# Two attentions with plain 64x64 products in place of folded weights, and roundings and a normalising moved to ScalarE

## What is computed

```python
# L2 and L3 attention: 8 heads of 64 channels
q, k, v = layernorm(x) @ Wq, context @ Wk, context @ Wv
out = softmax(q k^T / 8) v @ Wo + bo        # per sequence and head
x = x + tanh(g_xattn) * out
# L2 FFN, every linear layer with weights in {-1, 0, 1} and inputs rounded to 8 bits
act_quant(x): scale = 127 / clip(max|x|, 1e-5); round(x * scale) / scale
h = square(relu(bitlinear(y, w_gate))) * bitlinear(y, w_up)   # y = layernorm(x)
x = x + tanh(g_ffn) * bitlinear(h, w_down)
# L3 FFN: square(relu(y @ A)) @ B, with A and B prepared from ternary weights
```

## Time and profile before

| | us |
|---|---|
| median of 3 runs | 1649.75 (1649.02 to 1652.42) |
| the profiled execution's own time | 1648.05 |
| its span, first to last instruction | 1646.3 |
| TensorE busy in the span | 1494.6 |
| VectorE busy | 1190.2 |
| ScalarE busy | 874.5 |
| GpSimd busy | 582.6 |
| mean granted TensorE clock | 0.934 of full speed |

### The profile page before, as it was taken

How to read it: one execution, slowest core, us unless ns; L and a number is a source line. 1 busy time by engine, 2 the same in 40 slices (tenths; PEclk the granted TensorE clock), 3 DMA queues, 4 the chain that set the end, 5 groups by cost and what they waited for, 6 DMA issues and landing times.

```text
span 1646.3 us, 43347 instructions
## 1 busy us (share of the span) xinstructions
PE 1494.6 (91%) x14329; PEld 1046.6 (64%) x14329; DVE 1190.2 (72%) x4951; ACT 874.5 (53%) x1741; POOL 582.6 (35%) x1120
## 2 busy tenths in 40 slices
PE   6999999988998779898889689989988999899998
PEld 5888888875665445454477456656655665566665
DVE  6777877766777799999837744436888888865554
ACT  5656666654554555555323255555566666655543
POOL 4455544540000666666136411103322232222221
PEclk9999999998999687888669889999999999999999
DMA  8000000006200000000010000000000000000000
GB/s 191 2 0 0 0 0 0 0 2 138 52 0 14 1 0 0 0 0 0 2 46 0 15 19 0 0 0 2 1 2 0 0 1 1 2 8 7 6 13 20
DMA packets 40363, 22.41 MB, mean 14 GB/s; under 512 B 23231, under 2 KB 37790, under 8 KB 40158
## 3 DMA queue, kind: packets, MB, share of 16 engines
q1 hardware_dynamic: 40286, 21.42, 5.5%
HBM read 17.22 MB, written 4.19 MB: 13 GB/s over the span
## 4 chain that ended last, share of the span: by engine, by line
PE 63%; DVE 21%; issue 8%; ACT 4%; POOL 2%; DVEq 1%; DMA 0%; POOLq 0%; ACTq 0%
PE ps L681 7%; PE ps L690 7%; PE ps L2099 5%; PE ps L2094 5%; DVE arena L1355 5%; DVE arena L1349 4%; PE ps L303 3%; PE ps L310 3%; PE ps L352 3%; PE ps L332 3%; PE ps L2149 3%; PE ps L2160 2%; PE ps L343 2%; PE ps L323 2%; PE ps L2138 2%
## 5 line engine op out<-in xcount | busy, mean ns | idle before, releaser
L2262 ACT COPY arena<-ps 128x512 f32<-128x512 f32 x128 | 75.1, 587 | 150.9 <-PE ps L2099 150.9
L2094 PE MATMUL ps<-arena 128*128 128x128 f32 x1024 | 138.2, 281 | 3.4 <-ACT arena L2299 3.4
L681 PE MATMUL ps<-xnT,arena 128*128 128x512 f32 x256 | 135.1, 621 | 0.0
L2099 PE MATMUL ps<-arena 128*64 128x512 f32 x512 | 135.0, 605 | 0.0
L2094 PEld LDWEIGHTS ps<-arena 128*128 128x128 f32 x1024 | 126.8, 196 | 4.9 <-ACT arena L2299 4.4
L2557 POOL TENSOR_TENSOR arena<-arena 128x512 f32<-128x512 f32 x64 | 67.9, 1061 | 130.5 <-DVE arena L2493 130.0
L574 POOL TENSOR_TENSOR ln_veps<-ln_mv,eps 128x4 f32<-128x4 f32 x40 | 10.8, 269 | 269.0 <-DVE ln_mv L568 269.0
L1813 DVE TENSOR_SCALAR_CACHE_REDUCE thr_hits<-thr_abs,thr_candidate 128x512 bf16<-128x512 f32 (+1 forms) x248 | 101.8, 477 | 0.0
L1355 DVE MATCH_REPLACE8 arena<-arena 128x64 f32<-128x64 f32 x512 | 101.7, 210 | 0.1
L830 DVE SCALAR_TENSOR_TENSOR x_res<-ps,arena,x_res 128x128 f32 (+1 forms) x256 | 72.0, 345 | 31.1 <-PE ps L690 28.5
L2256 ACT COPY arena<-ps 128x512 f32<-128x512 f32 x128 | 77.1, 605 | 29.2 <-PE ps L2094 28.8
(11 more groups left out here) (409 smaller groups left out, 3978.4 us busy)
## 6 DMA issues: line engine op xcount, KB each, us to landing
toeplitz<-ssm_toeplitz_scratch SPq DMA_DIRECT2D x2, 2048.0 KB, 18.1
ssm_toeplitz_scratch<-ssm_padded_kernel SPq DMA_DIRECT2D x1, 2048.0 KB, 11.3
out<-x_res SPq DMA_DIRECT2D x8, 256.0 KB, 2.3
arena<-ctx SPq DMA_DIRECT2D x2, 768.0 KB, 6.0
arena<-L_ffn_W SPq DMA_DIRECT2D x2, 512.0 KB
arena<-L_xattn_Wq SPq DMA_DIRECT2D x1, 512.0 KB, 6.2
x_res<-x SPq DMA_DIRECT2D x1, 512.0 KB, 7.6
arena<-L_xattn_Wo SPq DMA_DIRECT2D x1, 512.0 KB, 8.2
```

The source lines that it names most:

```text
L681: nc.tensor.matmul(ps[:, u % 3, :], w1[:, x, c * P:(c + 1) * P], xnT, start=True, stop=True).then_inc(h_full.sem, 1)
L2094: last = T_.matmul(ps[:, 1 - n, j * P:(j + 1) * P], folded[phase].mT[:, 4 * n + j, :], cg[:, s, :], start=True, stop=True)
L2099: last = T_.matmul(ps[64 * m:64 * m + 64, 4, :], cg[:, s, b * CTX:(b + 1) * CTX], folded[phase].wvo[:, m, :, :], start=True, stop=True)
L2262: S.copy(VW[:, r % 2, b, :, :].rearrange("p c d -> p (c d)"), ps[:, 4, :]).then_inc(v_laid.sem, 1)
```

## The change

The function `fold_weights` is gone, with its work on TensorE, ScalarE and GpSimd ahead of the layer-1 FFN. `attention_weights` only loads the weights; ScalarE multiplies Wo and bo by the gate at the start of the decoder. A tile's attention now has queries and keys (4 products of 128x128 each), scores and heads (16 products of 64x64 each), values (4 products of 256 columns) and y. ScalarE rounds h and the normalised group, and normalises the four tiles; GpSimd computes the bias for that (-mean * 1/sqrt) and adds bo to x. The order of the streams changes.

```diff
-        k.fold_pool(e)      # and k.fold_act(e), k.fold_pe(e)
+def attention_weights(k, io, name, wq, wk, wv, wo, bo, inputs, outputs, conv_part):
+    def sp(e):
+        e.wait_ge(k.conv_done.sem, k.conv_done.at(conv_part))
+        e.dma_start(w.q, io[wq]).then_inc(w.loaded.sem, 16)
...
@@ pe_step @@
         if 2 <= r < STEPS + 2:
             e.wait_ge(p_laid.sem, p_laid.at(t - 1))
+            e.wait_ge(v_laid.sem, v_laid.at(t - 1))
+            e.wait_ge(q_laid.sem, q_laid.at(t + 1 if r < STEPS else STEPS))
+            for c, b_, m, rows, toks in quarters():
+                out = slice(64 * (m ^ b_), 64 * (m ^ b_) + 64)
+                last = T_.matmul(ps[out, 1 + b_, c * SEQ:(c + 1) * SEQ], VH[rows, s, b_, c, :], PT[rows, c, toks], start=True, stop=True)
+            last.then_inc(o_full.sem, 1)
+        if attend(r):
+            e.wait_ge(k_laid.sem, k_laid.at(t + 1))
+            for c, b_, m, rows, toks in quarters():
+                last = T_.matmul(ps[toks, 3 + m, c * CTX:(c + 1) * CTX], QT[rows, c, toks], KT[rows, c, toks], start=True, stop=True)
+            last.then_inc(s_full.sem, 1)
+            values(e, s, phase)
+        if 2 <= r < STEPS + 2:
+            e.wait_ge(o_laid.sem, o_laid.at(t - 1))
             for c in range(C):
                 for m in range(2):
+                    last = T_.matmul(ps[64 * m:64 * m + 64, 0, 0:D], OT[:, m, c, :], w_o[:, m, c, :], start=(c == 0), stop=(c == C - 1))
             last.then_inc(y_full.sem, 1)
+        if ahead(r, 1):
+            e.wait_ge(s_sub.sem, s_sub.at(t + 1))
+            turn_xn(e, t + 1, o)
         if gates(r):    # gate and up products, then x_done, hT, qT, PT's transpositions, queries, keys, down
...
@@ act_step @@
+        if downs(r):
+            e.wait_ge(a_recip.sem, a_recip.at(t - F2))
+            e.wait_ge(hq_done.sem, hq_done.at(t - F2 - 1))
+            S.activation(hq[:], h[:], ACT.Identity, bias=magic[:, 0:1], scale=sh[:, 0:1]).then_inc(hr_done.sem, 1)
+        if 2 <= r < STEPS + 2:
+            copy_heads(e, t)
+        if norms(r, 1):
+            e.wait_ge(n_shift.sem, n_shift.at(b))
+            for j in range(GT):
+                last = S.activation(k.xn[:, 0, j, :], k.x[:, tile_at(t, r, j, 7), :], ACT.Identity, bias=n_bias[:, j:j + 1], scale=k.rstd[:, 0, j:j + 1])
+            last.then_inc(n_out.sem, 1)
         if attend(r):
+            copy_values(e, t, s)
+            S.activation(PR[:, s, :, :, :], PR[:, s, :, :, :], ACT.Exp, scale=SCALE).then_inc(s_exp.sem, 1)
+        if ahead(r, 1):
+            copy_xn(e, t + 1, o)
         if gates(r):    # relu, hT's copy, qT's copy, PT's copy, square, then copy_queries, copy_keys
...
+        if norms(r, 2) and r < LN3:
+            for j in range(GT):
+                last = S.activation(qf[:, j, :], k.xn[:, 0, j, :], ACT.Identity, bias=magic[:, 0:1], scale=sc[:, j:j + 1])
@@ dve_step @@
         if downs(r):
-            round_h(e, t)
+            scale_h(e, t)        # scale and its inverse only
...              # maximum and subtraction of the scores, then:
+        if downs(r):
+            clip_h(e, t)
...              # after h and its maximum:
+        if downs(r):
+            e.wait_ge(y2_full.sem, y2_full.at(t - F2))
+            V.scalar_tensor_tensor(k.x[:, u, :], ps[:, 6, 0:D], yc[:, 0:1], k.x[:, u, :], ALU.mult, ALU.add).then_inc(y2_done.sem, 1)
@@ pool_step @@
+            G_.tensor_tensor(n_mean[:], k.mv[:, 0, :, 0], k.rstd[:, 0, :], ALU.mult).then_inc(n_mr.sem, 1)
+            G_.tensor_tensor(n_bias[:], n_zero[:], n_mean[:], ALU.subtract).then_inc(n_shift.sem, 1)
...
+            G_.tensor_tensor(xb, xb, weights[r // TILES].bo, ALU.add).then_inc(x_biased.sem, 1)
@@ build_program @@
-        fold2, w2 = fold_weights(..., 4)
-        fold3, w3 = fold_weights(..., 6)
+        load2, w2 = attention_weights(..., 8)
+        load3, w3 = attention_weights(..., 8)
```

More of the change, by code:

```diff
@@ L1910, in fold_weights @@
     w = Parts()
[L1911 removed]
+    INNER, C, half = 512, 4, 64
+    w.q, w.k, w.v, w.bo = inputs.f32(INNER), inputs.f32(INNER), inputs.f32(INNER), inputs.f32(D)
+    w.o = outputs.f32(2, C, D)
+    w.loaded, w.count = k.sem(name + "_w_loaded"), 112
     def sp(e):
         e.wait_ge(k.conv_done.sem, k.conv_done.at(conv_part))
[L1915 to L1965, removed]
@@ L1972, in decoder @@
+        halves = io[wo].rearrange("(c m p) d -> m p c d", m=2, p=half)
+        for m in range(2):
+            e.dma_start(w.o[half * m:half * m + half, 1, :, :], halves[1 - m]).then_inc(w.loaded.sem, 16)
+    return dict(sp=sp), w
+def decoder(k, io, weights, freed):
     nc, ps = k.nc, k.ps
@@ L2020, in decoder @@
     am, sc, cgt, cut = (cv.f32(GT) for _ in range(4))
+    n_zero, n_mean, n_bias = (cv.f32(GT) for _ in range(3))
     qf, qb, qT = cv.f32(GT, D), cv.bf16(GT, D), cv.bf16(GT * P)
@@ L2231, in pe_step @@
                 last.then_inc(o3_full.sem, 1)
-        if ahead(r, 1):
-            if turns_q(r):
-                e.wait_ge(qt_laid.sem, qt_laid.at(b - 1))
-            if turns_x(r):
-                e.wait_ge(x3_laid.sem, x3_laid.at(b - 9))
-            keys(e, t + 1, o, 1, (r + 1) // TILES)
     def pe(e):
+        for w in weights:
+            e.wait_ge(w.loaded.sem, w.loaded.at(w.count))
+            e.wait_ge(w_gated.sem, w_gated.at(4))
         e.wait_ge(before.sem, before.end)
-        for w in folded:
-            e.wait_ge(w.made.sem, w.made.end)
-        e.wait_ge(c_laid.sem, c_laid.at(1))
+        keys(e, 0, 0, 0)
         turn_xn(e, 0, 0)
-        keys(e, 0, 0, 0, 0)
-        keys(e, 0, 0, 1, 0)
+        queries(e, 0, 0, 0)
         steps(e, lambda t, r, b: pe_step(e, t, r, b))
@@ L2307, in act_step @@
         if ahead(r, 1):
-            copy_keys(e, t + 1, o, 1)
+            copy_queries(e, t + 1)
+            copy_keys(e, t + 1)
+        if norms(r, 2) and r < LN3:
+            g = b - 2
+            e.wait_ge(q_step.sem, q_step.at(4 * g + 3))
+            for j in range(GT):
+                last = S.activation(qf[:, j, :], k.xn[:, 0, j, :], ACT.Identity, bias=magic[:, 0:1], scale=sc[:, j:j + 1])
+            last.then_inc(q_step.sem, 1)
         if r == F3:
```

289 lines of the change are left out of this document (143 added, 146 removed).

## The result

The changed kernel takes 1637.79 us (median of 5 runs, 1634.22 to 1640.18); the kernel before, run beside it, 1651.22 (5 runs). The ratio is 0.9915, with a 95% interval of 0.9896 to 0.9935: faster by 0.85%, some 13 us where 29 were forecast. 1637.8 lies at the upper end of the range.

A forecast was written before the change was run, and what follows sets the result against it. TensorE bounds steps 2 to 9 and 44 to 62; in the L2 FFN TensorE and VectorE stop each other in turn. Terms -14 - 5 - 1 - 4 - 5 - 1.5 + 1.5 = -29 gave 1620 us, range 1594 to 1638.

The forecast's parts named there:

- Steps 2 to 9 and the start: Decoder's first steps: TensorE's demand of 53.4 us sinks by 5.6, taken as -5 (0 to -6); start -1 for 4 products.
- Rival B: L2 FFN: granted clock falls to 0.80, +11 us, 1631 in all; chance 0.13.
- L2 FFN: Steps 10 to 41: plain step 7.3 us, group of four 31.6 against 31.9, -4 in all (-46 to +24).
- wrong first if ScalarE's order let hq run earlier: Sign for the L2 FFN turn: hq running earlier than reckoned would upset the forecast first; half the range hangs on it.
- L3 FFN: Steps 44 to 62: TensorE stays full, step 7.98 becomes 7.3 us; -14 over 20 steps (-8 to -20).
- The middle term: Scores and heads, 16 products of 64x64 each, cost half of layer 0's: 0.63 and 0.58 us.
- Fold: Ahead of the layer-1 FFN: GpSimd's sum starts four us earlier, L1577 6.6 earlier; taken as -5 (-4 to -7).
- rival D: Layer-1 FFN stage: GpSimd and VectorE's loop hides the fold's time, 5 us less gain, 1625; chance 0.53 together with the forecast.
- Tail: Steps 64 and 65: last heads and their copy stand in the open, +1.5 us (0 to +3).
- A: L2 FFN: hq or the heads' copy do not hold y, group 28.8 us, -25 in all, 1599; chance 0.24.
- C: L2 FFN: ScalarE loop decides, slower, steps near 9 us, 1660 in all; extreme +82 from table loads; chance 0.07.

The follow-up runs named there:

- c1: The changed kernel with unread identity transpositions added on TensorE, 24 ahead of the decoder's first x and 14 in step 0; 1633.04 us, ratio 0.9901.
- s3: The changed kernel with exp's table loaded before the decoder and, in steps 0 and 1, the turned tile's copy ahead of the values' copy; 1635.36 us, ratio 0.9909.
- s4: The changed kernel with TensorE's wait for the previous step's x moved ahead of the keys, where nothing else writes that bank; 1636.06 us, ratio 0.9916.
- s1: The changed kernel with the heads' copy ahead of hq in ScalarE's order, nothing else; 1618.41 us, ratio 0.9803.
- d1: The changed kernel with hq, the rounding of h, moved from ScalarE back to VectorE; 1622.27 us, ratio 0.9843.
- f1: The changed kernel with GpSimd's four memsets put back ahead of its first sum in the stage behind the fold; 1641.99 us, ratio 0.995.
- n1: s1 with the four norms moved from ahead of the values' copy to the end of the ScalarE step; 1609.51 us, ratio 0.9752.
- d2: The changed kernel with hq, the four norms and the group's rounding all on VectorE as before; 1629.2 us, ratio 0.9874.

## Why the prediction was wrong

Of the 18 us by which the span fell short of the forecast of 29, the table shows 9.5 at the start, 4.65 in steps 2 to 9, 3.1 in the L2 FFN, 1.7 behind the fold and 0.7 in the tail; the untouched part gave 1.5 back.

**The step that failed is "Steps 2 to 9 and the start".** For the start it counted products, 4 fewer in the open, and wrote -1; it came to +8.5. What stood there instead: TensorE had new waits in its chain (the queries for the copy of the turned tile, 0.35 and 2.37 us; the scores for the copies of queries or keys, 0.72 and 0.77) and stayed at the lower granted clock for nearly all of 20.2 us, 0.55 in the mean, where the clock before was 0.90 over 17.2, at the lower level for a fifth of it. Rival B named this mechanism and put it in the L2 FFN, where the clock stayed at 1.00; at the start, where the clock already dipped, nobody priced it. c1 gives back 4.3 of it by filling TensorE and nothing else. The first exp with its table load in front of the turned tile's copy is another part; s3 alone gives back 2.7, of which 2.1 are the order. With s3, c1 and s4 the stretch is 19.3, still 2.1 over before: that rest is not explained by a run.

For steps 2 to 9 it took TensorE's demand as 53.4 - 5.6 = 47.8. The wait for x of the step before, moved by the change ahead of the transposed probabilities, stood in the open, 1.8 us of the stretch (s4). But even in s4 TensorE is busy 51.0 of 52.6. The groups of the replaced products in this stretch, scores, values and keys, were busy 41.1 us (16.9 + 15.9 + 8.3), and the new ones 37.2 (9.1 + 8.5 + 8.5 + 5.6 + 5.5), 0.49 a step less and not 0.70; and two gaps are open here that the L3 step covers with its FFN's second product: keys to heads 1.04 and not 0.90, heads to scores 0.79 and not 0.51. The price per step was taken from the L3 FFN and used in a stage that has no cover for the copies. How much of the remaining 3 us is which of the two, no run separates.

**L2 FFN: right, with sizes off and one place missed.** A plain step was to be 7.3 and is 7.6; the group's extras were to be 2.4 and are 1.4; the group 31.6 and 31.8. From h to hq a plain step takes 2.2 to 2.3, as reckoned (2.47 in the step in which VectorE puts the two group scales between), and from hq to y 1.34 where the terms give 1.4; what was too short is the way from y to the next h, 4.0 and not 3.7. hq takes 0.80 to 0.81 and the four norms 1.65 where the terms were 0.78 and 1.4. The Trainium skill (ScalarE: Activation LUTs, What ACT_TABLE_LOAD costs) has figures that give, as estimates, 0.80 for hq and 4 x 0.479 - 3 x 0.093 = 1.64 for the four norms; the trace agrees with both. The 1.5 that the prediction gave for the norms by that page was a slip: it is the row's 1.13 with four more operands, and not what the page's figures give.

By groups, the seven of steps 10 to 37 gained 3.6 us together, near the 4 forecast for all eight. The 3.1 that are missing lie in the last, steps 38 to 41, where the L3 FFN sets in: 34.87 against 32.07 before, with step 41 alone at 10.05. The forecast had no term for the L2 side of that border, and no run was made for it.

What was argued in one sentence, that h, scale, hq, copy and y stand strictly one behind another, is what s1 and d1 show: take hq out from ahead of the copy and 16 to 22 us of these steps are there. The forecast said that it would be wrong first if ScalarE's order let hq run earlier. It did not; the chain was as written.

**L3 FFN: right.** -13.85 against -14, TensorE busy throughout. The middle term, half of layer 0's price for half of its products, held: 0.58 and 0.51.

**Fold: right in kind, 1.7 short.** L1577 (L1575 now) starts 4.9 earlier behind the conv stage and not 6.6, since GpSimd's three sums took 1.76, 1.52 and 1.53 and not 1.26 each: they now run beside VectorE's, which take 1.56 in place of 0.69. A further 1.8 is lost in the stage's second tile: from the first activation to the second it is 8.9 us, as the next three intervals are in both kernels, where before's first was 7.1. So the loop of GpSimd and VectorE came some 3 us earlier and not 5. f1 shows that GpSimd's start carries all of it, so rival D, that the loop of the stage hides it, is out.

**Tail: near in number, by another cause.** It was to be +1.5 for the heads and their copy in the open in steps 64 and 65, and is +2.2. But from y of step 63 to y of step 65 it takes 10.06 where it took 10.74; the loss comes behind, from there to the end, 27.33 against 24.32. There the relu of the L3 FFN stands behind the four norms on ScalarE, which wait 2.17 us for GpSimd at 1615.8, and the clock is at its lower level for 3.4 us right after. With the norms at the end of the step (n1) or on VectorE (d2) it takes 24.3 again.

**Rivals.** A didn't come: hq did hold y. Under n1's order its time per group is reached (28.5). C didn't: the steps of the L2 FFN take 6.9 to 8.7 up to the border with L3, where one takes 8.9 and one 10.05, and there is one table load. The time of the result, 1637.8, is nearest to B's 1631, but the clock is 4.3 of the 18 us, and in another place than B's: the nearness is luck.

## What to carry to other kernels

Where an in-order engine gets a new instruction that waits, look first at what stands right behind it and who waits for that: here one swap of two instructions was worth 20 us, more than all the arithmetic saved in the L3 steps. A price per step read where an engine is full is only good where it is full; in the emptier stage price the gaps (a copy in the open, a moved wait) one by one. And at each place where a stage begins after a pause, ask what the granted clock does there when the engine has less to do than before.

## What the runs showed of the hardware

Sixteen products of 64x64, float32, whose four quarters differ in rows and output partitions, take 0.51 to 0.58 us from start to start at the full granted clock and 0.69 from the start of the first to the end of the last; at the lower clock 1.14 (the first scores of the decoder).

At the decoder's start, where TensorE waited 0.4 to 2.5 us ahead of several of its products, the granted clock was at its lower level for 20.5 us in seven of eight profiles and for 13.7 in the eighth; with the waits filled by products that nobody reads (c1) it was so for 3.4 us, and the useful work ended 4.3 us earlier. The Trainium skill (TensorE: Matmul & The Clock Gate, HAM oscillation — how this bites in real kernels) describes a kernel that loses time to the lower clock at waits for DMAs; here the waits are for ScalarE and VectorE, and a single stage start is enough.

VectorE's addition of two 128x512 tiles takes 0.69 alone and 1.56 when it starts beside GpSimd's addition of the same size, which itself goes from 1.26 to between 1.52 and 1.76. The Trainium skill (SBUF — State Buffer, SBUF: two separate sides) says that the two engines lock a shared port pair, each for a whole instruction, when VectorE reads two inputs from SBUF, and that the other one is blocked meanwhile. The trace agrees, with five additions in turn: VectorE's second ended at 845.77, 0.55 behind the end of GpSimd's first at 845.22; GpSimd's second at 846.89, 1.12 behind that; VectorE's third at 847.44, again 0.55 behind, and GpSimd's third at 848.57, 1.13 behind. Each takes a little less than its time alone after the other has ended.
